# Feed-forward: weights turned group by group between gate units, row chunks in turn, and the second gate integers begun by VectorE

## The reference

```python
x = act_qdq(x)                                  # one scale for the whole tensor: max|x| / 32767
up = act_qdq(x @ lpbq_dequant(w_up).T)          # weights: 4 bits, a scale for every 32 inputs
gate = act_qdq(x @ lpbq_dequant(w_gate).T)
sig = fixed_qdq_u16(jax.nn.sigmoid(gate))
gate = act_qdq(gate * sig)
o = act_qdq(gate * up)
return o @ lpbq_dequant(w_down).T
```

## Time and profile before

| | |
|---|---|
| three runs | 1581.59, 1581.92, 1583.39 us; median 1581.92 us |
| the profiled execution: its own time | 1582.63 us |
| the profiled execution: its span in the trace | 1580.8 us |
| busy over the span | PE 88%, DVE 67%, ACT 56%, POOL 50% |
| feed-forward part | from 1392.7 us to the end, 188 us |

### The profile page before, as it was taken

The page is one execution under the profiler, slowest core; times in us unless marked ns, Lnnn a source line. Parts: engine busy times, 40 slices in busy tenths (PEclk is TensorE's granted clock), DMA queues, the critical chain, the costliest instruction groups (busy, mean ns, idle before and its releaser), DMA issues. The chain is left out here.

```text
span 1580.8 us, 55267 instructions
## 1 busy us (share of the span) xinstructions
PE 1389.4 (88%) x24351; PEld 989.7 (63%) x24351; DVE 1061.8 (67%) x1681; ACT 881.5 (56%) x1195; POOL 789.2 (50%) x560
## 2 busy tenths in 40 slices
PE   4679999999999999999999999999997687459408
PEld 2457777777777777777777777777775355324107
DVE  7756666666666666666666666666664867785984
ACT  1445655665656565665556565656565565425742
POOL 4566555555655555555555555555530798420000
PEclk9899999999999999999999999999999898769859
DMA  4564444544444444444444444444421421010001
GB/s 150 145 137 137 107 107 110 128 120 120 117 127 132 107 107 116 121 124 122 114 136 121 107 107 120 124 124 114 117 65 53 131 54 27 1 41 0 1 0 54
DMA packets 90495, 155.97 MB, mean 99 GB/s; under 512 B 16704, under 2 KB 55496, under 8 KB 90256
## 3 DMA queue, kind: packets, MB, share of 16 engines
q1 hardware_dynamic: 88256, 150.92, 36.6%
q10 hardware_dynamic: 2000, 1.51, 0.4%
HBM read 60.95 MB, written 2.20 MB: 40 GB/s over the span
## 5 line engine op out<-in xcount | busy, mean ns | idle before, releaser
L645 DVE TENSOR_REDUCE MXP<-W_PS 128x1 f32<-128x512 f32 x768 | 510.7, 688 | 339.8 <-PE W_PS L456 338.7
L540 ACT ACTIVATE PR<-S_PS 128x1024 f32<-128x1024 f32 (+1 forms) x416 | 409.0, 1030 | 144.8 <-PE S_PS L404 142.8
L350 POOL TENSOR_TENSOR K_HI<-K,MCOL 128x512 f16<-128x512 f32 (+1 forms) x224 | 215.2, 961 | 282.8 <-ACT K L548 282.8
L356 POOL TENSOR_TENSOR CTX_LO<-CTX,CTX_HI 128x3202 f16<-128x3202 f32 x32 | 194.1, 6067 | 190.9 <-DVE CTX_HI L623 190.9
L456 PE MATMUL W_PS<-STK,QS 105*128 105x512 f16 (+1 forms) x1024 | 279.9, 336 | 10.1 <-POOL STK L377 6.1
L548 ACT ACTIVATE K<-W_PS,BK 128x512 f32<-128x512 f32 (+1 forms) x256 | 148.3, 593 | 175.9 <-PE W_PS L430 157.1
L404 PE MATMUL S_PS<-QS,STK 105*128 105x128 f16 (+1 forms) x3328 | 238.9, 220 | 4.2 <-ACT PR L540 2.9
L352 POOL TENSOR_TENSOR K_LO<-K,K_HI 128x512 f16<-128x512 f32 (+1 forms) x224 | 232.0, 1036 | 17.6
L404 PEld LDWEIGHTS S_PS<-QS,STK 105*128 105x128 f16 (+1 forms) x3328 | 210.4, 99 | 48.2 <-ACT PR L540 3.8
L439 PE MATMUL W_PS<-WV_HI,CTX_HI 128*128 128x256 f16 (+1 forms) x832 | 228.0, 274 | 2.8 <-ACT K L548 2.6
L439 PE MATMUL W_PS<-WV_HI,CTX_LO 128*128 128x256 f16 (+1 forms) x832 | 227.4, 273 | 0.0
(11 more groups left out here) (243 smaller groups left out, 1593.5 us busy)
## 6 DMA issues: line engine op xcount, KB each, us to landing
CTX<-in_ctx_t SPq DMA_DIRECT2D x64, 800.5 KB, 5.8
STK<-K_HI SPq DMA_DIRECT2D x256, 128.0 KB, 2.5
STK<-K_HI SPq DMA_DIRECT2D x256, 72.1 KB, 2.1
STK<-K_LO SPq DMA_DIRECT2D x128, 128.0 KB, 2.6
STK<-K_LO SPq DMA_DIRECT2D x128, 72.1 KB, 2.1
QSTK<-STK SPq DMA_DIRECT2D x12, 192.0 KB
SQS<-QK_HI SPq DMA_DIRECT2D x32, 64.0 KB, 2.2
X<-in_x SPq DMA_DIRECT2D x1, 1536.0 KB, 16.3
```

The source lines that it names most:

```text
L350: pool.tensor_tensor(K_HI[:, m, lo:hi], k32, zero, ALU.add).then_inc(k_hi, 1)
L356: pool.tensor_tensor(CTX_LO[:, u, :, :], CTX[:, :, :], CTX_HI[:, u, :, :], ALU.subtract).then_inc(ctx_lo, 1)
L540: nc.scalar.activation(PR[0:m, (NT * b + i) % PR_RING, :], S_PS[par][0:m, :], ACT.Exp).then_inc(p_sb, 1)
L645: dve.tensor_reduce(MXP[:, j, at:at + 1], bank[:, :], AX.X, ALU.max).then_inc(mx_done, 1)
```

## The change

Four edits, all in `feed_forward`.

1. `TURN` now maps a unit to one group. The four groups of w_up stand before gate units 12, 13, 14 and 15, and the six groups of w_down before units 16 to 21, on PE, ACT and DVE alike. `turn_weight`, `keep_weight` and `weight_low` do one group a call.
2. `place`: units 0 to 7 take slices 0 and 1 of chunk 0, then of chunk 1, and so on; units 8 to 23 are as before. It holds for gate and up units.
3. ACT makes four slices of up integers before it waits for `scales(3)`, then gate slice 1, up slice 4, gate slice 2, up slice 5, gate slices 3 to 5.
4. Gate slice 0 (`GI[:, 0]`) is rounded by DVE, right behind `scales(3)`.

```diff
-TURN = {8: 0, 16: 1}
+TURN = {12: (0, 0), 13: (0, 1), 14: (0, 2), 15: (0, 3),
+        16: (1, 0), 17: (1, 1), 18: (1, 2), 19: (1, 3), 20: (1, 4), 21: (1, 5)}
+UP_EARLY = 4
...
+    def place(i):
+
+        return (i % 2, i // 2) if i < 8 else (i // 4, i % 4)
...
-            if i < 4:
-                pe.wait_ge(sm["xt_lo"], i + 1)
+            if i < 8:
+                pe.wait_ge(sm["xt_lo"], i // 2 + 1)
             if i in TURN:
-                turn_weight(TURN[i])
+                turn_weight(*TURN[i])
...
-        for f in range(FT):
+
+        def up_integer(f):
+
             if f:
                 act.wait_ge(sm["ui"], f)
             nc.scalar.activation(up_int(f), U[:, f, :], ACT.Copy, scale=INV[:, 2:3]).then_inc(sm["ui"], 1)
+
+        for f in range(UP_EARLY):
+            up_integer(f)
         act.wait_ge(sm["sc"], 4 * SSTEPS)
-        for f in range(FT):
+        for f in range(1, FT):
             nc.scalar.activation(GI[:, f, :], G[:, f, :], ACT.Copy, scale=INV[:, 3:4]).then_inc(sm["g2i"], 1)
+            if UP_EARLY + f - 1 < FT:
+                up_integer(UP_EARLY + f - 1)
...
+        dve.tensor_scalar(GI[:, 0, :], G[:, 0, :], INV[:, 3:4], None, ALU.mult).then_inc(sm["giv"], 1)
+        dve.wait_ge(sm["giv"], 2)
         for f in range(FT):
-            dve.wait_ge(sm["g2i"], f + 1)
+            if f:
+                dve.wait_ge(sm["g2i"], f)
             dve.wait_ge(sm["ui"], f + 1)
             dve.tensor_tensor(G[:, f, :], GI[:, f, :], up_int(f), ALU.mult).then_inc(sm["ov"], 1)
```

More of the change, by code:

```diff
@@ L1502, in feed_forward @@
     SSTEPS = 5
+    def place(i):
+        return (i % 2, i // 2) if i < 8 else (i // 4, i % 4)
     def unit(t, i):
-        return t[:, i // 4, i % 4 * CH:(i % 4 + 1) * CH]
+        f, c = place(i)
+        return t[:, f, c * CH:(c + 1) * CH]
     weights = [(WUT, FT, KT), (WDT, KT, FT)]
@@ L1543, in _, with turn_weight @@
     def _(pe):
-        def turn_weight(w):
+        def turn_weight(w, e):
             dst, outs, ins = weights[w]
[L1547 to L1555, removed]
+            k, os = groups(w)[e]
+            n = WT_FIRST[w] + e
+            if e == 0:
+                pe.wait_ge(sm["w_val"], w + 1)
+            if n >= 2:
+                pe.wait_ge(sm["wt_lo"], n - 1)
+            for s, o in enumerate(os):
+                last = pe.transpose(WT_PS[n % 2][:, s * P:(s + 1) * P],
+                                    WN[w][:, (o * ins + k) * P:(o * ins + k + 1) * P], CST[:, C_ID:C_ID + P])
+            last.then_inc(sm["wt_ps"], 1)
         def spread(q):
@@ L1564, in inner @@
         def inner(bank, wt, ps, i):
-            f, c = i // 4, i % 4
+            f, c = place(i)
             parts = [(wt[0], 0), (wt[0], 1), (wt[1], 0)]
@@ L1615, in _, with keep_weight @@
     def _(act):
-        def keep_weight(w):
+        def keep_weight(w, e):
             dst, outs, ins = weights[w]
[L1619 to L1623, removed]
+            k, os = groups(w)[e]
+            n = WT_FIRST[w] + e
+            act.wait_ge(sm["wt_ps"], n + 1)
+            nc.scalar.activation(dst[0][:, k, os[0] * P:(os[-1] + 1) * P], WT_PS[n % 2][:, 0:len(os) * P], ACT.Copy,
+                                 scale=W_SCALE).then_inc(sm["wt_hi"], 1)
         for i in range(CHUNKS):
             if i in TURN:
-                keep_weight(TURN[i])
+                keep_weight(*TURN[i])
             act.wait_ge(sm["ga_ps"], i + 1)
@@ L1676, in weight_clip, with weight_low @@
             dve.tensor_scalar(WN[w], WN[w], -W_MAX - 1, W_MAX, ALU.max, ALU.min).then_inc(sm["w_clip"], 1)
-        def weight_low(w):
+        def weight_low(w, e):
             dst = weights[w][0]
[L1681 to L1686, removed]
+            k, os = groups(w)[e]
+            n = WT_FIRST[w] + e
+            cols = slice(os[0] * P, (os[-1] + 1) * P)
+            dve.wait_ge(sm["wt_hi"], n + 1)
+            dve.scalar_tensor_tensor(dst[1][:, k, cols], WT_PS[n % 2][:, 0:len(os) * P], W_SCALE, dst[0][:, k, cols],
+                                     ALU.mult, ALU.subtract).then_inc(sm["wt_lo"], 1)
         def scales(q):
@@ L1725, in _ @@
             if i in TURN:
-                weight_low(TURN[i])
+                weight_low(*TURN[i])
             dve.wait_ge(sm["ga_sb"], i + 1)
```

## The result

The changed kernel takes 1569.83 us in the median of four runs (1567.97 to 1570.41), the kernel before 1582.19 us (1581.59 to 1583.39): a ratio of 0.9919, with a 95% interval of 0.9902 to 0.9936, or 12.4 us. The forecast was 1570.4 us. The profiled execution took 1570.41 us with a span of 1568.6 us.

A forecast was written before the change was run, and what follows sets the result against it. Bounds: DVE's queue to PE's restart, then PE's list, later DVE waiting for ACT's gate slice. 7.47 + 4.04 = 11.51 us off 1582.63 gives 1571.1, less 0.7 for the median: 1570.4 us; range 1567.0 to 1574.5.

The forecast's parts named there:

- DVE's queue sets PE's restart, 2.38 us later than before: Gate stage: four more maxima stand ahead of the first low half on DVE, so PE restarts at 1421.86, not 1419.48.
- 5.3 us idle before unit 14: Gate stage: PE reaches the first low half's wait at 1416.6 and idles 5.3 us, until 1421.86.
- Edit 2 is worth nothing: Gate units 0 to 7: the new chunk order's microsecond lies inside PE's idle time, so alone it gains nothing.
- the slow start behind the restart takes 6.29 us: Behind PE's restart: the clock falls in the idle time; six transposes and units 14 and 15 take 6.29 us, as before.
- Eight units and twelve transposes in 12.16 us, without waits: Gate units 16 to 23 with w_down's groups: units at 1.295 us (10.36), transposes at 0.15 us (1.80), no waits.
- First stage 7.47 us: Up to the first up unit, from groups between gate units: it starts at 1440.31 instead of 1447.78, 7.47 us earlier.
- Second stage 4.04 us: Second gate integers (edits 3, 4): DVE's first product starts at 1508.20, 4.04 us earlier, with DVE staying the path.
- All of it reaches the end: Behind the last gate maximum everything moves along, so 7.47 us reach the end; with 4.04 us the sum is 11.51.
- the first did not come: Rival at PE's restart: the clock does not fall or recovers sooner, 1567.4 to 1569.4 us; chance 0.16.
- recover late: Rival behind PE's restart: clock stays at 0.50 longer, 1582.6 us if through units 16 to 23; chance 0.06.
- ran in lockstep: Rival behind PE's restart: each of seven groups waits 0.4 us, 2.8 us lost, 1573.2 us; chance 0.08.
- both halves reached the end: Rival on the two stages: only one half's gain works, 1577.9 us without the first, 1574.5 without the second; chance 0.08.

The follow-up runs named there:

- the second: The changed kernel run once more, unaltered, as a control in another group: 1569.59 us, ratio 0.9911.

## Why the prediction was right

- *DVE's queue sets PE's restart, 2.38 us later than before.* Right: E to R went from 26.36 to 28.74 us, 2.38 us, and moving DVE's low halves moved it (25.18). Six more profiles have 28.74 or 28.75.
- *5.3 us idle before unit 14.* 5.94 us in the first profile, 5.38 us in the second. The restart was in its place; PE came sooner to it in the first, where the clock rose 3.0 us behind E and not 5.2 us as in the profile of before.
- *Edit 2 is worth nothing.* Right, shown alone and by undoing it. E to U was 45.51 to 46.14 us in three profiles with it, which idle for 5.38 to 5.94 us, and 45.39 and 45.40 us in two without, which idle for 4.40 and 4.41 us; the medians (1569.59 and 1569.83 with it, 1570.59 without) lean the other way, so no cost is shown.
- *The clock falls, and the slow start behind the restart takes 6.29 us.* It fell, as forecast, in every profile with a wait of 4.40 to 5.94 us here, 2.3 to 4.7 us behind PE's last matmul (in two of them just behind the restart). The start was somewhat shorter: six transposes and two units took 1427.92 - 1422.19 = 5.73 us. With transposes in the wait, the clock held at 1.00, they take 3.30 us, so the fall costs 2.43 us. That the same start would return was the weak step: read in stretches of 0.25 us, the clock was back 5.0 us behind the restart in this profile, 4.9 us in one more of these five and 3.6 to 3.7 us in three; with the old gate groups 6.1 us in two profiles (that of before among them) and 3.7 to 3.8 us in two. The stretch from restart to U follows it, with the same list on PE: 28.3 us in the first two, 27.1 us in the others, and half of 6.1 - 3.7 us is these 1.2 us.
- *Eight units and twelve transposes in 12.16 us, without waits.* No waits, and 11.67 us (1427.92 to 1439.59). A unit with two transposes takes 1429.65 - 1428.13 = 1.52 us, so two transposes cost 0.22 us and not 0.30 us. The 0.15 us each were a misreading of a row: 0.60 us for four holds the end of the last one, which overlaps what follows. In the new profile a row of two transposes lasts 0.38 us, and the next matmul starts after 0.21 us (1427.92, 1428.13). Without some 0.16 us of such an end, four cost 0.44 us, 0.11 us each, and so do 48 in a row (5.40 us).
- *First stage 7.47 us.* 8.52 us in the profile; the two terms above are the 1.05 us.
- *Second stage 4.04 us.* 4.01 us, and no product of DVE waits. That the whole of it hangs on DVE's slice 0, with ACT's new order as a second way to the same end, the prediction did not say.
- *All of it reaches the end.* Yes: U to P fell by the second stage's gain alone, and P to S is 68.56 us in both. The sum was 11.51 us against 12.53 us from E to S in the profiles (187.68 to 175.15).
- *The rivals.* The clock fell, so the first did not come. It did not recover late either: with groups between units it was at 1.00 from about 1427.2, short of the 1429 that would have been a sign against the forecast. That transposes do not hold the clock up, the rule behind this rival, failed in the test. Nothing ran in lockstep (no wait behind the restart), and both halves reached the end.
- *How near the number came.* The forecast of 1570.4 us is 0.6 us above the median, and 11.5 us of gain stand against 12.4. The mechanism was right, but a hit this close is partly luck: with nothing else changed, the profiles with the same gate stage differ by how soon the clock rises, and the first stage is worth 7.3 to 9.3 us by which profile of the old groups (E to U 53.44 to 54.66) is set against which of the new ones (45.39 to 46.14).

## What to carry to other kernels

When a wait is moved, look at what stands ahead of the releasing instruction in its own engine's list: here six maxima on DVE stood ahead of the first low half, and putting two low halves ahead of them brought 5 us more, two fifths of what the whole change had. Two edits that shorten the same wait do not add; time each alone before keeping both. An idle stretch of PE on the path costs its length and, where the clock falls, half of the slow stretch behind it: 1.7 to 2.4 us here behind waits of 4.40 to 5.94 us, and 1.7 us behind some waits of under 3 us.

## What the runs showed of the hardware

In the last product PE's wait for DVE left the clock at 1.00 in eight profiles (2.06 to 2.53 us) and was followed by 1.7 us of loss in four (2.61 to 2.82 us), while in the gate stage of the changed kernel it stood at 1.00 through the whole of two waits of 4.40 and 4.41 us, and fell 2.3 us into one of 5.38 us. Length alone does not settle it. Transposes of f32 tiles held a clock that was at 1.00 there for 5.4 us, as matmuls did, and cost 0.11 us each in a row. Behind identical code, the start of the feed-forward part lay between 1392.1 and 1395.7 us, which is as much as the smaller edits bring; marks within the stage, and not the total, tell these apart.
